# Routing plan of 15 tiles copied one body sooner, second normalisation half on ScalarE, scores by chunk, and first results loaded ahead of gathered rows

## What is computed

```python
x = x + xattn(layernorm(x), ctx, ctx, mask)      # relu(q Wq + b), relu(k Wk + b), relu(v Wv + b)
                                                 # scores = relu(qp kp^T) / sqrt(512) + mask; out = relu(scores vp)
z = layernorm(x)
logits = z @ gate_w                              # [2, 2048, 8]
topv, topi = top_k(logits, 2)
w = softmax(topv)
Y = (silu(z @ Wu[e]) * (z @ Wv[e])) @ Wo[e]      # for the two experts e of a token
out = x + sum_k w_k * Y_k
```

## Time and profile before

| | us |
|---|---|
| median of 3 runs | 429.07 |
| lowest, highest | 428.71, 431.38 |
| profiled execution | 429.35 |
| its span, first to last instruction | 427.6 |
| granted TensorE clock, mean | 0.991 |

### The profile page before, as it was taken

The page is one execution under the profiler, slowest core; times in us unless marked ns, Lnnn a source line. Parts: engine busy times, 40 slices in busy tenths (PEclk is TensorE's granted clock), DMA queues, the critical chain, the costliest instruction groups (busy, mean ns, idle before and its releaser), DMA issues.

```text
span 427.6 us, 10469 instructions
## 1 busy us (share of the span) xinstructions
PE 404.1 (94%) x3063; PEld 359.5 (84%) x3063; DVE 344.8 (81%) x1126; ACT 267.5 (63%) x581; POOL 194.5 (45%) x231
## 2 busy tenths in 40 slices
PE   8999999999999999998989889999999998999990
PEld 5698988998889988888778778888999997899970
DVE  2679899999999999999767878778887767888760
ACT  1677877778778777776667656666666443344430
POOL 2011135556655555554546743333333154666641
PEclk9999999999999999999999999999999999999996
DMA  8812235877767677544766868779964689999830
GB/s 288 266 64 70 92 100 202 286 270 255 250 219 240 230 258 260 191 152 159 236 236 194 302 190 278 246 232 304 280 205 104 221 271 366 387 368 400 320 137 36
DMA packets 53622, 97.98 MB, mean 229 GB/s; under 512 B 8384, under 2 KB 19136, under 8 KB 53440
## 3 DMA queue, kind: packets, MB, share of 16 engines
q1 hardware_dynamic: 41648, 63.21, 46.4%
q0 software_dynamic: 11920, 34.10, 21.0%
HBM read 54.15 MB, written 50.80 MB: 245 GB/s over the span
## 4 chain that ended last, share of the span: by engine, by line
PE 55%; DVE 23%; ACT 7%; issue 5%; DMA 3%; SPq 2%; POOL 1%; POOLq 0%; DVEq 0%; ACTq 0%
PE psQ L1531 9%; PE psQ L1532 9%; PE psQ L1533 9%; PE psT L1527 6%; DVE st L1138 4%; DVE x L1127 4%; PE psS L1531 3%; DVE qpT L955 2%; PE psQ L1527 2%; PE psO L1531 2%; PE psZ L1533 2%; PE psZ L1531 2%; PE psO L1532 2%; PE psO L1533 2%; PE psZ L1532 2%
## 5 line engine op out<-in xcount | busy, mean ns | idle before, releaser
L955 DVE TENSOR_TENSOR qT<-psT,qT 128x512 fp32r<-128x512 f32 x103 | 69.4, 688 | 25.5 <-ACT qT L751 25.4
L1531 PE MATMUL psQ<-wuv,qT 128*128 x284 | 86.4, 304 | 0.0
L657 POOL DMA_INDIRECT z_dram<-zb x64 | 70.9, 1108 | 31.3 <-issue 15.3
L1532 PE MATMUL psQ<-wuv,qT 128*128 x284 | 80.2, 283 | 0.0
L1533 PE MATMUL psQ<-wuv,qT 128*128 x284 | 80.1, 282 | 0.0
L1531 PE MATMUL psQ<-qT,wq 128*128 128x256 f32 x256 | 75.1, 294 | 0.0
L1533 PE MATMUL psQ<-qT,wq 128*128 128x256 f32 x256 | 72.4, 283 | 0.0
L1532 PE MATMUL psQ<-qT,wq 128*128 128x256 f32 x256 | 72.4, 283 | 0.0
L751 ACT ACTIVATE qT<-psT 128x512 fp32r<-128x512 f32 x103 | 59.5, 594 | 15.2 <-PE psT L1527 15.2
L1531 PEld LDWEIGHTS psQ<-wuv,qT 128*128 128x128 f32 x284 | 53.7, 189 | 3.0
L1532 PEld LDWEIGHTS psQ<-wuv,qT 128*128 128x128 f32 x284 | 54.0, 190 | 0.0
(11 more groups left out here) (325 smaller groups left out, 1050.5 us busy)
## 6 DMA issues: line engine op xcount, KB each, us to landing
wq<-z_dram SPq DMA_DIRECT2D x42, 264.0 KB, 4.0
xin<-in_x_dram SPq DMA_DIRECT2D x11, 512.0 KB, 4.6
z_dram<-spare SPq DMA_DIRECT2D x17, 264.0 KB, 4.6
qpT<-z_dram SPq DMA_DIRECT2D x17, 264.0 KB, 3.8
acc_dram<-spare SPq DMA_DIRECT2D x17, 256.0 KB, 4.8
xin<-acc_dram SPq DMA_DIRECT2D x16, 256.0 KB, 4.8
vp<-acc_dram SPq DMA_DIRECT2D x12, 256.0 KB, 5.3
kpT<-z_dram SPq DMA_DIRECT2D x10, 264.0 KB, 3.4
```

What stands on the lines that cost most here:

```text
L657: pool.indirect_dma_start(out=z_dram, out_offset=bass.IndirectOffsetOnAxis(ap=z_of(b)[:, t, ROW_COL + k:ROW_COL + k + 1].bitcast(U32), axi ...
L955: nc.vector.tensor_tensor(o, a, b, ALU.subtract).then_inc(s, 1)
L1531: pe.matmul(o, w[LO], a[HI], start=first, stop=False)
L1532: pe.matmul(o, w[HI], a[LO], start=False, stop=False)
```

## The change

- `norm_x` is no longer called in the bodies; ACT makes both tiles of xn (`norm1(nxt, 0)`, `norm1(nxt, 1)`).
- `keep_stats` stands behind `turned_x` on DVE.
- `scores` waits before chunk c for the low half of that chunk only.
- `turn_logits` transposes the strips as they are, and a new TENSOR_REDUCE on DVE adds them into `logits` in SBUF, from which MAX and MAX_INDEX now read. `gates` waits for it (`folded`).
- `EARLY_NB` is 11: part 0 has tiles 0 to 14, its plan is made in body 13, turned and copied in body 14; part 1 begins with tile 15.
- In the tile stage the plan's steps stand one iteration later: lengths 8, ends 9, rows 10, `keep_sched(1)` with `know_pads` and `plan_used(1)` 11; the `lists_*` steps 12 to 19, `keep_sched(2)` 21, `keep_kinds` 22. PE's turns stand behind tiles 10 and 20.
- On SP `load_acc` stands ahead of `load_z`, `copy_tail` behind it, and the order of first results is shifted by one.

```diff
-EARLY_NB = 12
+EARLY_NB = 11
...
+        ps_strips = psG[:, 0:BT].rearrange("p (t c s) -> p t s c", t=TPB, s=STRIP)[:, :, 0:E, :]
...
             for t in range(TILES):
-                if EARLY <= t < EARLY + E:
-                    if t == EARLY:
-                        sp.wait_ge(pads_known, 2)
-                        sp.wait_ge(head_stored, 16 * E)
-                    copy_tail(t - EARLY)
...
-                load_z(t)
                 if t >= bulk:
                     for a in accs[t]:
                         load_acc(a)
+                load_z(t)
+                if EARLY <= t < EARLY + E:
+                    if t == EARLY:
+                        sp.wait_ge(pads_known, 2)
+                        sp.wait_ge(head_stored, 16 * E)
+                    copy_tail(t - EARLY)
...
                 else:
+                    norm1(nxt, 0)
                     norm1(nxt, 1)
...
                     ge(dve, logit_turned, self.b.n + 1)
+                    nc.vector.tensor_reduce(logits[:, :, :], ps_strips, AX.X, ALU.add).then_inc(folded, 1)
+                    ge(dve, folded, self.b.n + 1)
...
-                    norm_x(nxt)
...
-                ge(pe, qp_lo, 4 * b.n + 4)
...
                 for c in range(DC):
+                    ge(pe, qp_lo, 4 * b.n + c + 1)
...
-                    ins = pe.matmul(ps_logit[:, t, :], logT[:, t * P:(t + 1) * P], pick[:, :], start=True, stop=True)
+                    ins = turn(ps_log[:, t * P:(t + 1) * P], logT[:, t * P:(t + 1) * P])
```

More of the change, by code:

```diff
@@ L200, in moe_block @@
         logT = sb("logT", [P, BT])
+        logits = sb("logits", [P, TPB, E])
         top_v = sb("top_v", [P, TPB, 8])
@@ L571, in _ @@
             bulk = FIRST_B + RING - 1
[L572 to L573 removed]
+            todo = [FIRST_B + LATE, *range(FIRST_B, FIRST_B + LATE), *range(FIRST_B + LATE + 1, TILES)]
+            accs = {bulk - 1: [todo.pop(0) for _ in range(5)]}
             for t in range(bulk, TILES):
[L575 removed]
+                accs[t] = [todo.pop(0) for _ in range(2 if t in (bulk, bulk + 4) else 1)]
             accs[TILES] = todo
             for t in range(TILES):
[L578 to L582 removed]
                 if FULL + 2 <= t < FULL + 2 + E:
@@ L1391, in body @@
                     norm2.shift()
-                    keep_stats(prv)
                 for t in range(TPB):
@@ L1397, in body @@
                         turned_g(t)
+                if prv.real:
+                    keep_stats(prv)
                 if ends_early:
@@ L1727, in body @@
                     gates(old)
-                if not nxt.real:
+                if b.n == EARLY_NB + 3:
                     pe.wait_ge(sched_ready, 2)
```

60 lines of the change are left out of this document (28 added, 32 removed).

## The result

The changed kernel takes 437.17 us in the median (436.35 to 437.88, 4 runs) where the kernel before, run beside it, takes 428.89 (428.29 to 431.38). The ratio is 1.0182, with a 95% interval from 1.0144 to 1.022: **1.8% slower**. The prediction was 432.0 with a range of 428.5 to 435.5, so the time lies outside it. The profiled execution took 437.55, its span is 435.8, 8.2 more than before's 427.6.

What follows compares the result with a forecast made beforehand. PE and DVE, both nearly full, were taken to bound the bodies, PE alone the tiles. The first tile's -2.0 turned into +4.7 by tile 25; with -1.8 for first results, +2.9 on 429.07 gave 432.0 us, range 428.5 to 435.5.

Steps and rivals of the forecast that it cites:

- Steady bodies, -2.5: Bodies up to 13: the DVE and ACT loop gives a period of 11.63, not 11.86, over 11 periods: -2.5 us.
- rival B: Bodies: ACT closes the loop at the old period of 11.86, the 2.5 are not won: 434.5 us; chance 0.17.
- First two bodies, +0.8: First two bodies: second xn on ACT delays each by up to 0.70, scores by chunk return some: +0.8 (0 to 1.4).
- Plan of part 0, +0.3 in bodies 13 and 14: Plan steps of 3.05 move into bodies 13 and 14, all paid: periods 14.68 and 11.2, +0.3 for the two.
- body 15, -0.6: Body 15: tile 0's load no longer waits for block 11's scatter, nor PE for a plan: -0.6 (0 to -1.0).
- Copy of part 1 and SP's pace, +6.7 between tile 13 and 25: Tiles 13 to 25: part 1 copied about 250.2, then SP's load-and-copy pairs of 3.24 make PE wait: 6.7 us lost.
- The forecast's 253.6: Tile 15: the time PE wants its rows, which land at 255.3, a stall of 1.7.
- rival D: Tiles 15 to 23 or 26 to 34: landings slower than 3.8 with PE right behind, +2 to +3, 434.5 us; chance 0.13.
- Rival A: Tiles from 15: SP's pace stays hidden, pairs take 2.67 and the plan's copy comes 2 us sooner: 424.4 us; chance 0.10.
- -2.0 from the bodies: Start of the first tile: 0.8 - 2.5 + 0.3 - 0.6 makes it begin 2.0 us sooner.
- First results, -1.8: Late tiles: the 1.7 wait for a first result goes, a held-tile wait of 1.2 comes, later ones shrink: -1.8 (0 to -3.1).
- rival C: Bodies: PE bounds the period at 11.45, for example if MAX and MAX_INDEX are shorter from SBUF: 430.0 us; chance 0.15.

Runs made afterwards that it cites:

- e_pool: The changed kernel with POOL making the next block's rstd ahead of the gap's exponent in the bodies: 435.86 us, ratio 1.0152.
- b_pool: The kernel before with only POOL's swap (next block's rstd ahead of the gap's exponent): 457.07 us beside 458.93 for before, ratio 0.9974.
- e_z01_again: The changed kernel with loads of tiles 0 and 1 ahead of expert 7's weights in SP's last body but one, second run: 438.6 us, ratio 1.0218.
- b_stall_n22: The kernel before with 22 extra unread TENSOR_REDUCE in DVE's iteration 40, making PE wait: 459.61 us beside 455.12 for before, ratio 1.01.
- b_stall_n10: The kernel before with 10 extra unread TENSOR_REDUCE in DVE's iteration 40, making PE wait: 458.01 us beside 455.12 for before, ratio 1.0073.
- e_copies_last: The changed kernel with all eight tail copies behind the load of tile 24, not one behind each load of tiles 15 to 22: 438.2 us, ratio 1.0203.
- best1_again: The kernel before with the body's edits, POOL's rstd ahead of the gap's exponent and the new order of first results, second run: 427.9 us, ratio 0.9961.
- b_early11: The kernel before with only EARLY_NB = 11, so 15 tiles in part 0 and its plan one body sooner: 432.67 us, ratio 1.0065.
- e_plan_sooner: The changed kernel with the plan's steps in the tile stage back at the iterations of before, still 15 tiles in part 0: 433.82 us, ratio 1.0098.
- e_early12_ahead: The changed kernel with 17 tiles in part 0 and each tail's copy ahead of its load again: 431.72 us, ratio 1.0084.
- best2: best1_again with the plan's steps in the tiles one iteration later, 17 tiles in part 0 and copies ahead of loads: 429.79 us, ratio 1.0017.
- e_early12: The changed kernel with 17 tiles in part 0 again (EARLY_NB = 12), plan steps later and copies behind the loads: 435.33 us, ratio 1.0112.
- b_body_pool: The kernel before with the body's edits and POOL's rstd ahead of the gap's exponent: 428.88 us beside 429.0 for before, ratio 0.998.
- b_body: The kernel before with only the body's edits; plan, tiles and SP's order as before: 430.62 us beside 429.0 for before, ratio 1.0016.

## Why the prediction was wrong, point by point

**Steady bodies, -2.5: the step that failed is the list of loops.** DVE-and-ACT's loop was walked to 11.63, and the period measures 11.65 once POOL is out of the way. But nothing was said on where rstd comes from. It is made on POOL behind four scatters and the gap's exponent, and in the kernel before that loop was hidden under DVE's 11.86. The period became 11.82, and 0.4 was won in nine periods in place of 2.1. (An eleventh period of the sum does not exist, so the term was 0.2 too large by its own rule.) The result looks like rival B, an old period that stays, but not by its mechanism: e_pool has the same ACT program and a period of 11.65.

**First two bodies, +0.8:** 0.46 up to mask 3, inside the bounds. Over all traces this mark stands at 64.39 to 65.82 with the body's edits and at 63.72 to 64.22 without them (65.05 in b_pool), so that 0.8 was a fair size. **Plan of part 0, +0.3 in bodies 13 and 14, and body 15, -0.6:** the two bodies were to take 14.68 and 11.2 and take 13.97 and 12.54, which is +0.60 against before's 11.83 and 14.08; body 15 takes 12.25 in place of 12.06, +0.2. Against two periods of 11.82 the plan costs 2.87, near the 3.05 of the walk, but nothing of it was hidden or made good in the second period, where 11.2 was forecast. In body 15 PE waits 1.06 for tile 1; the step had the load freed from its old wait for the scatter and left out the weights of expert 7 that it stands behind on SP. e_z01_again says that the other order of these loads wins nothing.

**Copy of part 1 and SP's pace, +6.7 between tile 13 and 25: right in kind, too small.** What was forecast is there: one load 1.24 after the copy (1.27 forecast), pairs of 3.35 (3.24), PE waits at tile 15 and on, a second wait of about 2 at tile 25. Measured are 9.43. Along the forecast's own walk the size that fails is the step from the load of tile 23 to PE's transposes of it: 3.8 forecast, a landing with PE waiting for it, and 5.33 measured (280.75 to 286.08). PE waits for nothing there; it is still behind from the wait of 2.34 at tile 20 and the lower clock after it, and the eight pairs took 0.8 more than forecast. Of the 2.7 more, 1.70 is that lower clock, in no term of the sum, and shown by b_stall_n22 to be a price of its own. The other 1.0 was not measured apart; a short wait can cost more than its length, 0.27 in b_stall_n10, and whether that is it stays open. (The forecast's 253.6, when PE wants tile 15, does not follow from the terms beside it; measured it is 256.10, 2.5 later, where the first tile is 2.8 later than forecast.) The wait of 2.34 is in part rival D in small: the load of tile 20 was issued at 270.69 in the row of pairs and landed 5.16 later, where the median is 3.8. Rival A, the pace hidden, is out: removing the copies between the loads (e_copies_last) removed the waits.

**The share of each part of the change there** was not in the prediction at all, which took the later plan for a shift that -2.0 from the bodies would pay. Tiles 13 to 25 take:

| | 17 tiles | 15 tiles |
|---|---|---|
| plan as before, copies ahead | 33.50 (before), 33.52 (best1_again) | 36.08 (b_early11) |
| plan as before, copies behind | | 36.51 (e_plan_sooner) |
| plan later, copies ahead | 36.39 (e_early12_ahead), 37.06 (best2) | |
| plan later, copies behind | 41.02 (e_early12) | 42.93 (after), 42.70 (e_z01_again), 41.57 (e_pool) |

The fewer tiles cost 2.6 alone and the later plan 2.9 (3.5 from best1_again to best2). The third edit, the copies behind the loads, has no run of its own: on top of the fewer tiles it costs 0.4, on top of the later plan 4.6, where the last copy's landing stands in the way of part 2 and the clock falls. With the other two in place the fewer tiles cost 1.9, less than alone, and the later plan 6.4, of which 1.7 is the lower clock; against e_pool, which has no lower clock, it is 5.1. So what multiplies is the later plan with the copies behind the loads, and not the fewer tiles. That the ring's lead covers part of each alone and little of the two would explain it; this is argued from the walk, not shown, and fewer tiles with a later plan and copies ahead were not run. The bodies' gain that was to pay for it was not there, and where it was, in e_pool, with its first SiLU 2.51 sooner, the waits stayed (five of 1.11 to 1.71): DVE's plan moves along with the tiles, so that an earlier front does not buy the copy any lead.

**First results, -1.8:** -1.17 from tile 25 on, in its bounds (0 to -3.1). The forecast's wait for a held tile came, at 1.4 in place of 1.2, and the later ones did not all go. Alone it gives less still, 0.5.

**What was said to show it:** period near 11.63: no. First tile 2 sooner: no, 0.83 later. Copy near 250: 252.75, by the 2.8 of the first tile's miss, less 0.3 that the tiles made good. Waits of `turn_g` named after `z_dram`, a second wait at 25: yes. Tiles of 3.2: not evenly, 2.9 to 4.2 from tile 13 to 18, then one of 6.7. The sum of the misses, in the order of the first table: -0.1 and +1.7 in the bodies, +1.1 up to the first tile, -0.9 in tiles 0 to 13, +2.7 in 13 to 25, +0.6 behind, +0.2 for the eleventh period: 5.3.

## What to carry to other kernels

Before you book a gain on the engine that is full, walk every loop that returns to the same instruction, slack engines included: an engine that is busy 59% of a period can hold it, and a loop that lies 0.05 below the old period caps the gain. A transfer that a later stage needs in full is placed by where its landing is wanted, not by where its issue disturbs least. And edits that eat the lead of one ring have to be priced together: the plan one iteration later costs 2.9 with the copies ahead of the loads and 5.1 to 6.4 with fewer tiles and the copies behind them, and a wait of about 2 may cost the clock behind it as well.

## What the runs showed of the hardware

- PE's clock after waits: 0.50 behind 2.34 (the changed kernel), 3.35 (b_stall_n22), 3.38 (e_early12) and 5.9 (e_copies_last), and also behind 1.75 (e_z01_again) and 1.91 (b_body_pool); full behind 1.03, 1.14 and 1.28, and also behind 1.80 (the changed kernel), 1.98 (e_pool), 2.12 (best2), 2.37 (b_body) and 2.77 (b_stall_n10). So waits from 1.75 to 2.77 ended either way, and the length of the one wait does not decide; what does is open. The price was 1.7 to 1.83 beyond the wait where it was read off in a trace, and 1.9 in the times of b_body_pool.
- POOL's scatter of 128 rows takes 0.96 to 1.69 with 0.30 between two of them, and the first starts 0.74 after the semaphore that it waited for; four of them and that start are 6.4 in a row on one engine.
- A pair of load and copy with its three register reads takes SP 3.22 to 3.30 in six of eight cases of the changed kernel with nothing in it to wait for, 3.69 in the first and 3.48 in the last; 3.24 in the mean of seven in the kernel before. A register read takes 0.28 of it in the median (the 71 reads of row numbers, 0.26 to 1.09). The floor from the Trainium skill, "DMA: Bandwidth & Descriptors", Latency and other measured facts, on which the prediction's sentence behind the pairs rests, does not show in these reads.
- MAX and MAX_INDEX on eight columns take nearly the same time from SBUF as from PSUM. The groups of the kernel after (busy us, mean ns of one), where before has 160 and 165 ns with `psG` as input:

```profile
L1184 DVE FIND_INDEX8 top_i<-top_v,logits 128x8 uint32<-128x8 f32 x32 | 4.7, 160 | 0.0
L1179 DVE MAX8 top_v<-logits 128x8 f32<-128x8 f32 x32 | 3.8, 160 | 0.5
```

The difference of access times from the Trainium skill, "Perfetto Trace Analysis", Optimizing Scalar/DVE Operations, on which the prediction's sentence beside rival C rests, does not show in these rows. Nor does it in MATCH_VALUE_LOAD, the third instruction that moved: 82 ns from either.
